# Attention and a sign-weight gate on one core: the planner of the instruction order learns when the copy of a chunk's sums is done

## The chip, the cores and the metric

One core of one Trainium2 chip runs the whole kernel in one launch. The metric is the device time of a run in microseconds (us); three runs of the kernel before are shown. A profiled execution gives the trace.

## The reference

The input x is 4 batches of 2048 tokens with 256 channels, in float32. It is normalised by token (xn). Two branches read xn: masked attention with 16 heads of 16 channels, in which query i sees keys j >= i, and a three-layer network with weights of +1 and -1, whose output passes through silu. The result is x plus the product of both branches.

```
qkv = xn @ w_qkv + b_qkv                      # 16 heads of 16
scores = q k^T / 4, and -inf where j < i
s = (softmax(scores) v, heads joined) @ w_out + b_out
h = [xn, -xn]
h = relu(s0 * h @ K0) * 2                     # K = where(k, 1, -1); to 1024
h = relu(s1 * h @ K1) * 2                     # 1024 to 1024
g = silu(s2 * h @ K2)                         # 1024 to 256
out = x + s * g
```

## The kernel before

Two phases follow each other. In the first, normalise_and_project (about the first 200 us), the tokens are normalised, q, k and v are computed chunk by chunk (a chunk is 512 tokens) and stored to scratch tensors. The second phase, attend_and_combine, holds the change.

The second phase has 16 groups (one batch, four heads), and each group goes through its four chunks of queries from the last to the first. One step is one block of 128 keys against one chunk of queries for the four heads: 4, 8, 12 and 16 steps for the four chunks, 40 a group, 640 in all. The work of TensorE (PE) has these kinds:

- **M**, the maxima: a matmul pair of queries by keys (line 1283) into two of the seven banks of ps; VectorE reads them and keeps the largest value of each row (lines 1435 and 1438). They belong to the group ahead. Once a chunk's maxima are there, they are transposed (line 1291) and written into an extra row of the queries.
- **S**, the scores: a matmul pair of keys by queries (line 1271) into two banks; ScalarE turns them into probabilities by an exponential (line 1383), kept in one of four slots of probs. Steps on the diagonal are masked on GpSimd (line 1177).
- **PV**, the products: probs times values (line 1303), accumulated over a chunk's steps in the single bank pv_ps. The fourth row group holds the sums of the softmax. After the chunk's last step, "out" on ScalarE copies pv_ps to sums_T (line 1393), from where DMAs store it ("keep"). The next chunk's first product overwrites the same bank, so it waits for that copy (semaphore out_done).
- **F**, the network: matmuls of 256 columns over 32 pieces of 256 tokens, layers L0 (line 1322), L1 (line 1325) and L2 (line 1329). Each "use" fills one bank; ScalarE reads it (relu in line 1411 for L0 and L1, an exponential and a copy in lines 1403 and 1404 for L2), and GpSimd splits a relu's output into a high and a low part (lines 1205 and 1207). After L2 come eight reciprocals on VectorE (line 1461, "recip") and one product on GpSimd (line 1215, "gate"), which makes way for the next L2's values on ScalarE.

After a batch's heads are done, its chunks are combined: loads ("fetch", "fetch_heads"), "bias" and "scale" on GpSimd, "invert" on VectorE (line 1471), "project" on PE (line 1348), then a store. For the last batch this stands in the last group.

The order of all this is one list for all engines. The class Plan makes it while the program is built: it keeps a clock for each engine and a time at which each bank is released, and at every turn it chooses among R (an S or an M pair), V (a step of PV) and F (network matmuls, two at a time, in stretches of 12 or more). The chip does not see those clocks; it sees the order, and semaphores make it safe. Each engine carries out its own part of the list in order. Three rules of the choice matter here:

```
    def products_from(self):
        t = self.products
        return self.probs_at[t] if t < self.scores // 2 else float("inf")
...
        if t == TOTAL or t >= self.products + P_SLOTS:
            return float("inf")
...
        late = behind > 0 and self.scores // 2 > TOTAL - STEPS
```

The first says from when a product may be chosen. The second is that scores run at most four steps ahead of the products. The third sets in with the last group: where the network is behind its even share of the whole, F goes on without a limit to its stretch.

Of the kernel before, what the change touches and what calls it, by code (L numbers as in the profile page):

```python
# [11 lines left out]
ACT = mybir.ActivationFunctionType  # L12
# [7 lines left out]
CHUNK = 512  # L20
# [576 lines left out]
class Plan:  # L597
# [17 lines left out]
    def __init__(self):  # L615
# [13 lines left out]
        self.probs_at, self.rows_at = {}, {}  # L629
        self.turns = []  # L630

    def emit(self, what, *args):
        self.out.append((what, *args))
        return len(self.out) - 1
# [107 lines left out]

    def products_from(self):
        t = self.products
        return self.probs_at[t] if t < self.scores // 2 else float("inf")

    def take_scores(self):
        t, pair = divmod(self.scores, 2)
# [30 lines left out]
    def take_products(self):  # L779
        g, s = divmod(self.products, STEPS)  # L780
        c, _, cols, _, stop = self.steps[s]
        self.emit("PV", g, s)
        self.clock["PE"] += 4 * cols / self.STREAM
        self.products += 1
        if stop:
            self.emit("out", g, c)
            self.clock["ACT"] = max(self.clock["ACT"], self.clock["PE"] + self.SEEN) + 0.5
            self.later(self.step() + 1, 0.0, "keep", g, c)

    def take_network(self, count):  # L790
        kind, k, q, total = self.uses[self.use]
        if self.done == 0:
            if kind == "L1" and q in (0, 2) and k + 1 < PIECES:

                self.end_span()
                self.emit("load_x" if q == 0 else "split_x", k + 1)
                self.clock["POOL"] += 0.0 if q == 0 else 1.9
            self.take(("F", self.use), "f")
        bank = self.banks["F", self.use][0]
        count = min(count, total - self.done)  # L800
        lo, self.done = self.done, self.done + count
        if self.span:
            lo = self.span[6]
        end = self.done == total
        self.span = (self.use, self.split, self.needed.get((kind, k), 0), k, kind, q, lo, self.done, end)
        self.clock["PE"] += 0.1177 * count
        self.matmuls += count
        if not end:
            return
        self.end_span()  # L810
        if kind == "L2":
            self.release[bank] = self.reads("ACT", self.clock["PE"], self.EXP, 1400)
            self.clock["POOL"] = max(self.clock["POOL"], self.release[bank]) + 1.0
            t = self.step()
            per = 2 if k + 1 < PIECES else SIG_PARTS
            for part in range(SIG_PARTS):
                self.later(t + 2 + part // per, 0.3 + 2 * (part % per) / per, "recip", k, part)
            self.later(t + 2 + SIG_PARTS // per, 0.6, "gate", k)
        else:
            if self.split >= U_SLOTS:  # L820
                self.clock["ACT"] = max(self.clock["ACT"], self.split_at[self.split - U_SLOTS])
            self.release[bank] = self.reads("ACT", self.clock["PE"], self.EXP, 640)
            self.clock["POOL"] = max(self.clock["POOL"], self.release[bank]) + 1.95
            self.split_at.append(self.clock["POOL"] + 0.1)
            self.split += 1
            self.needed["L1" if kind == "L0" else "L2", k] = self.split
        self.use += 1
        self.done = 0
# [705 lines left out]
```

## Time and profile before

| | before |
|---|---|
| median of three runs | 2479.2 us (2477.48 to 2480.41) |
| the profiled execution's own time | 2475.66 us |
| its span | 2473.9 us |
| PE busy | 2368.8 us, 96% of the span |
| VectorE busy | 1801.0 us, 73% |
| ScalarE busy | 1529.0 us, 62% |
| GpSimd busy | 910.8 us, 37% |
| mean granted clock of PE | 0.98 of full speed |

The profiled execution lies 3.5 us below the median; 1.8 us of its time lie outside the span. Busy time is the union of an engine's instructions. A matmul's end is modelled, so the start of one matmul to the start of the next says more than its duration. In the chain of work that ended last, rows of PE follow on one another, so the start of one row to the start of the next is what that stretch of matmuls took.

### The profile page before, as it was taken

The page shows a single profiled execution, that of the slowest core. Times are in us where ns is not written, and L with a number is a line of the kernel's source. Part 1 is how long each engine was busy: PE and PEld are TensorE (multiplying, and loading weights), DVE is VectorE, ACT ScalarE, POOL GpSimd, SP SyncE. Part 2 cuts the span into 40 slices and gives each one's busy share as a digit, 9 for nine tenths or more (in the row PEclk, how much of TensorE's full clock was granted, in tenths as well). Part 3 has the DMA queues.
Part 4 walks back from the last instruction along what each step waited for, and adds up shares of the span by engine and source line. Part 5 has one row for each costly group of instructions (what it writes and reads, how often), then busy time and mean ns, then how long its engine had stood idle before and what let it go on. Part 6 is the DMA issues. An engine that isn't in the chain of part 4 may idle for free.

```text
span 2473.9 us, 50994 instructions
## 1 busy us (share of the span) xinstructions
PE 2368.8 (96%) x17616; PEld 1491.4 (60%) x17616; DVE 1801.0 (73%) x4516; ACT 1529.0 (62%) x3135; POOL 910.8 (37%) x1080
## 2 busy tenths in 40 slices
PE   7999999999999999999999999999999999999885
PEld 6786655565556666656656666655666665666542
DVE  7767777777878777777777777777777777777622
ACT  5654566666666665666666665666666666666552
POOL 1004333233334344442435343442435343443432
PEclk9999999999999999999999999999999999999986
DMA  8993111110212112121312122121312121121321
GB/s 307 355 335 87 31 39 50 30 53 25 53 32 81 46 42 80 47 76 38 90 40 75 43 53 73 44 76 38 90 43 72 43 81 51 38 75 46 96 86 53
DMA packets 157805, 192.67 MB, mean 78 GB/s; under 512 B 65276, under 2 KB 102076, under 8 KB 157560
## 3 DMA queue, kind: packets, MB, share of 16 engines
q1 hardware_dynamic: 156600, 189.41, 25.1%
q8 instruction: 152, 2.49, 0.4%
q14 instruction: 93, 0.76, 0.1%
q10 hardware_dynamic: 960, 0.00, 0.0%
HBM read 112.13 MB, written 76.14 MB: 76 GB/s over the span
## 4 chain that ended last, share of the span: by engine, by line
PE 88%; DMA 4%; DVE 2%; ACT 2%; issue 2%; POOL 1%; SPq 1%; POOLq 0%; ACTq 0%; DVEq 0%
PE b_ps L1325 21%; PE b_pv_ps L1303 21%; PE b_ps L1283 15%; PE b_ps L1271 15%; PE b_ps L1329 5%; PE b_ps L1322 5%; PE b_ps L1348 3%; DMA a_xs<-L_attn_x 2%; ACT b_probs L1383 2%; PE a_qk_ps L290 1%; DVE a_stats L396 1%; DVE a_qk_parts L434 1%; PE a_v_ps L300 1%; DMA b_xs<-L_attn_x 1%; PE b_ps L1291 0%
## 5 line engine op out<-in xcount | busy, mean ns | idle before, releaser
L1383 ACT ACTIVATE b_probs<-b_ps 128x512 f32<-128x512 f32 (+3 forms) x2560 | 1187.0, 538 | 673.3 <-PE b_ps L1271 658.4
L1438 DVE TENSOR_REDUCE b_part_max<-b_ps 128x1 f32<-128x512 f32 x1536 | 964.2, 682 | 286.9 <-PE b_ps L1283 280.9
L1303 PE MATMUL b_pv_ps<-b_probs,k_vst 128*32 128x512 f32 (+3 forms) x5120 | 584.9, 542 | 48.6 <-ACT b_probs L1383 32.8
L1435 DVE CUSTOM_DVE_ANT_0 b_ps<-b_ps,k_mask 128x512 f32<-128x512 f32 (+3 forms) x1024 | 476.8, 520 | 210.2 <-PE b_ps L1283 208.0
L1325 PE MATMUL b_ps<-b_u_hi,k_w 128*128 128x256 f32 x2048 | 541.8, 300 | 0.1
L1271 PE MATMUL b_ps<-k_qst,k_kst 50*128 50x512 f32 (+3 forms) x2560 | 509.0, 413 | 3.3 <-DVE b_part_max L1435 2.5
L1325 PE MATMUL b_ps<-b_u_lo,k_w 128*128 128x256 f32 x2048 | 502.4, 281 | 0.0
L1283 PE MATMUL b_ps<-k_kst,k_qst 48*128 48x512 f32 (+3 forms) x2560 | 491.4, 409 | 3.4 <-DVE b_part_max L1438 0.9
L1325 PEld LDWEIGHTS b_ps<-b_u_hi,k_w 128*128 128x128 f32 x2048 | 390.6, 191 | 84.8 <-issue 79.7
L1205 POOL CAST b_u_hi<-b_u 128x512 fp32r<-128x512 f32 x256 | 156.8, 612 | 707.0 <-ACT b_u L1411 706.7
L1283 PEld LDWEIGHTS b_ps<-k_kst,k_qst 48*128 48x128 f32 x2560 | 235.4, 186 | 278.9 <-issue 146.1
L1325 PEld LDWEIGHTS b_ps<-b_u_lo,k_w 128*128 128x128 f32 x2048 | 389.8, 190 | 0.7
L1271 PEld LDWEIGHTS b_ps<-k_qst,k_kst 50*128 50x128 f32 x2560 | 245.3, 186 | 237.2 <-ACT b_probs L1383 73.1
L1207 POOL TENSOR_TENSOR b_u_lo<-b_u,b_u_hi 128x512 fp32r<-128x512 f32 x256 | 328.9, 1285 | 21.0
L1177 POOL TENSOR_SCALAR_AFFINE_SELECT b_probs<-b_probs 128x512 f32<-128x512 f32 x256 | 162.4, 635 | 325.6 <-ACT b_probs L1383 324.6
L1411 ACT ACTIVATE b_u<-b_ps,k_sign 128x512 f32<-128x512 f32 x256 | 176.6, 692 | 151.9 <-PE b_ps L1325 107.6
L1303 PEld LDWEIGHTS b_pv_ps<-b_probs,k_vst 128*32 128x32 f32 x5120 | 110.2, 108 | 228.1 <-issue 142.8
L1435 DVE DVE_READ_ACCUMULATOR2_ANT b_part_max<- 128x1 f32 x1024 | 144.1, 141 | 0.0
L1329 PE MATMUL b_ps<-k_w,b_u_hi 128*128 128x256 f32 x512 | 137.3, 303 | 0.0
L1322 PE MATMUL b_ps<-b_x_hi,k_w 128*128 128x256 f32 x512 | 133.7, 297 | 1.2 <-POOL b_x_lo L1195 1.1
L1329 PE MATMUL b_ps<-k_w,b_u_lo 128*128 128x256 f32 x512 | 125.9, 281 | 0.0
L1461 DVE RECIPROCAL b_sig<-b_sig 128x64 f32<-128x64 f32 x256 | 121.9, 518 | 5.2 <-POOL b_sig L1200 5.2
(101 smaller groups left out, 1852.9 us busy)
## 6 DMA issues: line engine op xcount, KB each, us to landing
qk_parts<-a_qk_parts SPq DMA_DIRECT2D x64, 512.0 KB, 4.0
k_kst<-qk_parts SPq DMA_DIRECT2D x384, 64.0 KB, 2.3
k_qst<-qk_parts SPq DMA_DIRECT2D x384, 64.0 KB, 2.3
a_xs<-L_attn_x SPq DMA_DIRECT2D x16, 512.0 KB, 5.8
xn_T<-a_xT SPq DMA_DIRECT2D x16, 512.0 KB, 5.5
v_plain<-a_v_out SPq DMA_DIRECT2D x16, 512.0 KB, 5.4
k_xf<-xn_T SPq DMA_DIRECT2D x32, 256.0 KB, 3.6
b_v_in<-v_plain SPq DMA_DIRECT2D x64, 128.0 KB, 2.6
```

The costliest lines, as they stand in the source:

```text
L1177: pool.affine_select(out=at, in_=at, pattern=[[0, GH], [-1, P]], compare_op=ALU.is_ge, fill=0.0, base=0, channel_multiplier=1).then_inc(ma ...
L1207: pool.tensor_tensor(u_lo[:, tiles], u[:, split % U_SLOTS], u_hi[:, tiles].bitcast(F32), ALU.subtract).then_inc(u_split, 1)
L1271: pe.matmul(outs[half][:, 0:cols], keys, qst[rows, c, pair, 0:cols], start=True, stop=True).then_inc(s_ready, 1)
L1283: pe.matmul(outs[j], qst[rows, c, pair, i * P:(i + 1) * P], kst[rows, k_slot(kc, g % 2), pair, k1:CHUNK], start=True, stop=True).then_inc( ...
L1303: mm = pe.matmul(pv_ps[h * VW:(h + 1) * VW, 0:cols], vst[:, kb // TT, kb % TT, h, :], probs[:, s % P_SLOTS, h, 0:cols], start=start, stop= ...
L1322: mm = pe.matmul(dst[:, tile], kept.w0[:, f, m * P:(m + 1) * P], (x_hi, x_lo)[part][:, f, :], start=first, stop=last)
L1325: mm = pe.matmul(dst[:, tile], kept.w1[:, f, m * P:(m + 1) * P], (u0_hi, u0_lo)[part][:, f, :], start=first, stop=last)
L1329: mm = pe.matmul(dst[:, tile], (u1_hi, u1_lo)[part][:, f, tile * P:(tile + 1) * P], kept.w2[:, f, :], start=first, stop=last)
L1383: act.activation(probs[:, s % P_SLOTS, h, 0:cols], ps[:, banks[place, half][0], 0:cols], ACT.Exp, scale=HD ** -0.5).then_inc(exp_done, 1)
L1411: act.activation(u[:, split % U_SLOTS], f_bank(use), ACT.Relu, scale=kept.sign[:, layer:layer + 1]).then_inc(f_read, 1)
L1435: dve.tensor_tensor_reduce(src, src, mask[:, 0:CHUNK - k0 % CHUNK], 1.0, -3.0e38, ALU.add, ALU.max, dst).then_inc(ring_read, 1)
L1438: dve.tensor_reduce(dst, src, AX_X, ALU.max).then_inc(ring_read, 1)
```

## The change

The plan gets a time `copied`, at which ScalarE's copy of a chunk's sums is done by its own clocks, and no product is chosen before it. It used to add a fixed 0.5 to ScalarE's clock and to hold no product back. A second edit stands in the network's part: at the start of every L2 use, all reciprocals and gates of the piece before that are still listed for later are put out at once. Nothing that any engine computes is different; only the order is.

```diff
@@ class Plan, __init__
+        self.copied = 0.0
@@ products_from
         t = self.products
-        return self.probs_at[t] if t < self.scores // 2 else float("inf")
+        return max(self.probs_at[t], self.copied) if t < self.scores // 2 else float("inf")
@@ take_products
         if stop:
             self.emit("out", g, c)
-            self.clock["ACT"] = max(self.clock["ACT"], self.clock["PE"] + self.SEEN) + 0.5
+            self.copied = self.reads("ACT", self.clock["PE"], self.EXP, CHUNK)
             self.later(self.step() + 1, 0.0, "keep", g, c)
@@ take_network
                 self.emit("load_x" if q == 0 else "split_x", k + 1)
                 self.clock["POOL"] += 0.0 if q == 0 else 1.9
+            if kind == "L2":
+
+                self.end_span()
+                for event in [e for e in self.side if e[2] in ("recip", "gate")]:
+                    self.side.remove(event)
+                    self.emit(*event[2:])
             self.take(("F", self.use), "f")
```

The lines of the changed kernel stand 8 lower: products are line 1311, maxima 1291, scores 1279, L1 1333, L2 1337, exponentials 1391, the copy 1401, relu 1419.

Two places show what the order becomes. The first is PE's order in the twelfth group (batch 2), where the chunk with eight steps ends and the chunk with twelve begins. Before:

```order
7295 L1271 MATMUL b_ps<-k_qst,k_kst 128x512 x2
7296 L1283 MATMUL b_ps<-k_kst,k_qst 128x512 x2
7297 L1271 MATMUL b_ps<-k_qst,k_kst 128x512 x2
7298 L1303 MATMUL b_pv_ps<-b_probs,k_vst 32x256 x4
7299 L1303 MATMUL b_pv_ps<-b_probs,k_vst 32x512 x4
7300 L1283 MATMUL b_ps<-k_kst,k_qst 128x512 x2
```

and with the change:

```order
7097 L1279 MATMUL b_ps<-k_qst,k_kst 128x512 x2
7098 L1291 MATMUL b_ps<-k_kst,k_qst 128x512 x2
7099 L1311 MATMUL b_pv_ps<-b_probs,k_vst 32x256 x4
7100 L1279 MATMUL b_ps<-k_qst,k_kst 128x512 x2
7101 L1291 MATMUL b_ps<-k_kst,k_qst 128x512 x2
7102 L1279 MATMUL b_ps<-k_qst,k_kst 128x512 x2
7103 L1311 MATMUL b_pv_ps<-b_probs,k_vst 32x512 x4
```

The first chunk's last product (256 columns) and the next chunk's first (512 columns) followed each other; now three pairs, two of scores and one of maxima, stand between them.

The second place is ScalarE's order where the last group begins, up to the copy of the group before it (the exponentials of 128 columns belong to the last group's second step). Before:

```order
883 L1411 ACTIVATE b_u<-b_ps,k_sign 128x512
884 L1383 ACTIVATE b_probs<-b_ps 128x384 x2
885 L1383 ACTIVATE b_probs<-b_ps 128x256 x4
886 L1411 ACTIVATE b_u<-b_ps,k_sign 128x512
887 L1383 ACTIVATE b_probs<-b_ps 128x512 x4
888 L1393 ACTIVATE b_sums_T<-b_pv_ps 128x512
889 L1383 ACTIVATE b_probs<-b_ps 128x128 x4
```

and with the change:

```order
863 L1391 ACTIVATE b_probs<-b_ps 128x512 x4
864 L1419 ACTIVATE b_u<-b_ps,k_sign 128x512 x8
865 L1411 ACTIVATE b_sig<-b_ps,k_gate_scale 128x512
866 L1412 ACTIVATE b_z<-b_ps,k_gate_scale 128x512
867 L1391 ACTIVATE b_probs<-b_ps 128x128 x2
868 L1401 ACTIVATE b_sums_T<-b_pv_ps 128x512
869 L1391 ACTIVATE b_probs<-b_ps 128x128 x2
```

Eight relus and one L2's two readings now stand there in one piece, without an exponential among them: on PE this is a stretch of 186 network matmuls (the rest of one L1 use, three more, four L0 uses and an L2 use), and after four pairs of maxima, two of scores and two products another of 84. The first is the only place of the program where the second edit puts anything out: eight reciprocals and a gate stand ahead of that L2.

Counted over the whole of PE's order:

| | before | with the change |
|---|---|---|
| chunk ends after which the next product follows at once (of 63) | 20 | 0 |
| stretches of scores and maxima (R) | 975 | 998 |
| stretches of products (V) | 525 | 584 |
| stretches of network matmuls (F, with transposes and projections) | 510 | 486 |
| network matmuls that stand in the last group | 288 | 538 |

## Rows read from the trace of the kernel before

**Rows 1.** The page: span and busy times of the engines.
```profile
span 2473.9 us, 50994 instructions
PE 2368.8 (96%) x17616; PEld 1491.4 (60%) x17616; DVE 1801.0 (73%) x4516; ACT 1529.0 (62%) x3135; POOL 910.8 (37%) x1080
```
**Rows 2.** Waits of PE, 230 to 2360 us: in total, times, longest.
```profile
PE b_pv_ps L1303 <- ACT b_probs L1383: 32.8, 21, 1.9
PE b_ps L1271 <- DVE b_part_max L1435: 2.5, 1, 2.5
PE b_pv_ps L1303 <- ACT b_sums_T L1393: 0.9, 1, 0.9
```
**Rows 3.** Timeline of PE around 1775 us: start us, us, instruction [idle before].
```profile
1773.66 0.64 PE L1303 MATMUL b_pv_ps<-b_probs,k_vst 128*32 128x256 f32 x8
1775.98 1.07 PE L1303 MATMUL b_pv_ps<-b_probs,k_vst 128*32 128x512 f32 x8 [1.68 <-ACT b_probs L1383]
```
**Rows 4.** Timeline of ScalarE at the same place.
```profile
1773.33 2.06 ACT L1383 ACTIVATE b_probs<-b_ps 128x512 f32<-128x512 f32 x4 [0.29 <-PE b_ps L1271]
1775.25 0.63 ACT L1393 ACTIVATE b_sums_T<-b_pv_ps 128x512 f32<-128x512 f32 x1
```
**Rows 5.** The chain of work, 1746 to 1789 us: start us, us, what.
```profile
1747.85 0.99 PE b_pv_ps L1303 x8
...
1753.59 0.43 PE b_ps L1283 x2
1754.02 0.23 PE b_ps L1271 x2
1754.25 0.23 PE b_ps L1283 x2
1754.48 1.00 PE b_pv_ps L1303 x8
...
1769.91 0.43 PE b_ps L1271 x2
1770.34 0.66 PE b_ps L1283 x4
1771.00 0.67 PE b_ps L1329 x4
...
1783.20 1.85 PE b_pv_ps L1303 x16
...
1785.73 1.61 PE b_ps L1325 x12
```
**Rows 6.** Timeline of PE: the second and the last of twelve network matmuls.
```profile
1077.05 0.28 PE L1329 MATMUL b_ps<-k_w,b_u_lo 128*128 128x256 f32 x1
...
1078.22 0.28 PE L1329 MATMUL b_ps<-k_w,b_u_lo 128*128 128x256 f32 x1
```
**Rows 7.** Busy time by stretch: stretch, length, PE, PEld, DVE, ACT, POOL busy, clock, DMA.
```profile
1500.00:2000.00 500.00, 494.89 (x3774) 304.50 (x3771) 379.28 (x948) 321.73 (x664) 196.85 (x232) 0.99 0.20 57
```
**Rows 8.** Groups of the costliest instructions: busy, mean ns, idle before.
```profile
L1207 POOL TENSOR_TENSOR b_u_lo<-b_u,b_u_hi 128x512 fp32r<-128x512 f32 x256 | 328.9, 1285 | 21.0
L1411 ACT ACTIVATE b_u<-b_ps,k_sign 128x512 f32<-128x512 f32 x256 | 176.6, 692 | 151.9 <-PE b_ps L1325 107.6 <-PE b_ps L1322 25.3 <-POOL b_u_lo L1207 17.9
L1205 POOL CAST b_u_hi<-b_u 128x512 fp32r<-128x512 f32 x256 | 156.8, 612 | 707.0 <-ACT b_u L1411 706.7
L1215 POOL TENSOR_TENSOR b_gt<-b_z,b_sig 128x512 f32<-128x512 f32 x32 | 41.1, 1285 | 6.2 <-DVE b_sig L1461 6.2
```
**Rows 9.** The chain of work where the last group begins.
```profile
2290.27 4.65 DMA b_sums<-sums
...
2294.94 0.55 DVE b_sums L1471
```
**Rows 10.** Waits of PE, 2360 us to the end.
```profile
PE b_ps L1348 <- POOL b_heads_T L1237: 19.3, 3, 8.0
PE b_pv_ps L1303 <- POOL b_probs L1177: 14.3, 3, 7.6
```

## The prediction

> **What bounds the kernel now.** I read the page first, for who is busy: PE for 2368.8 of 2473.9 us, VectorE for 73% and ScalarE for 62% of it [rows 1]. PE is the bound, and the other two have slack on the average. Then PE's waits, for what PE could win: between 230 and 2360 us it waits for 36.2 us altogether in the three largest rows, and 33.7 of them, in 22 waits, stand before a product (line 1303) [rows 2]. The row names ScalarE's exponentials (line 1383), and that name has to be looked at closely. The timeline at one such place shows it: PE ends the eight matmuls of a chunk's last product at 1774.30, then sits idle for 1.68 us until the next chunk's first product at 1775.98 [rows 3]. ScalarE has four exponentials in its queue until 1775.39, and behind them the copy of pv_ps from 1775.25 to 1775.88; the product starts 0.10 after the copy's end [rows 4]. So it is the copy (line 1393) that PE waits for, and the exponentials are what the copy waits behind. The 22 waits fit the 20 chunk ends at which the order has nothing between the two products, with two or three where it has too little. Last I read the chain of work, from start to start, for what the stretches of matmuls cost.
>
> **Term 1, the waits removed.** All 20 places get other work: in the first place shown, three pairs, 0.9 us. The 33.7 us go, as far as the filler is long enough: −33.7.
>
> Some fillers are short. After the change seven chunk ends have only two to four pairs in between (0.7 to 1.1 us by the pairs of [rows 5]), where the wait from the last product's end was 1.7. That leaves 0 to 1.0 us at each of seven, 0 to 7; since the plan holds the product back by a clock that counts ScalarE's queue, I take +2.
>
> **Term 2, more and shorter stretches.** Work that is taken in between cuts other stretches. PE's order has 59 more stretches of products, 23 more of scores and maxima, and 24 fewer of the network. What each costs is read from the chain. One step of products takes 0.99, two in a row 1.85, not 1.98 [rows 5]: a stretch more costs 0.13. Three pairs take 0.43, 0.23 and 0.23 [rows 5]: the first pays 0.20. Twelve network matmuls take 1.61 [rows 5], and from the second to the last start of twelve it is 1.17 for ten intervals [rows 6], 0.117 each, so 1.40 without the change of kind: 0.21. The sum is 59 × 0.13 + 23 × 0.20 − 24 × 0.21 = 7.7 + 4.6 − 5.0 = +7.3. On each of these edges the trace shows the lost time beside the row, whatever its reason. The Trainium skill (TensorEngine Tiling (Array Packing), Key Properties) has a rule that speaks against this change: changing the tiling mode drains TensorE. Its page on TensorE (TensorE: Matmul & The Clock Gate, Single matmul latency) gives a fixed part of a warm matmul's latency of 398 cycles at 2.4 GHz, 166 ns; with a full drain at each of the 58 more changes of kind, an estimate by these two pages is 9.6 us, and the sum would be 2.3 us less of a gain. The rows give 7.3, and the trace agrees that each change is paid for.
>
> **Term 3, thinner groups.** The network falls behind: 538 instead of 288 of its matmuls stand in the last group, so the 15 groups before it have 250 fewer, 250 × 0.117 = 29.3 us of PE work moved later. That is neutral as long as PE stays the bound in those groups. But the same maxima and scores then have less filler between them, and seven banks to go round. VectorE is busy for 379 of 500 us there and ScalarE for 322 [rows 7], so with 2 us less of filler a group (137 us) neither is near its limit on the average; what can come is the short wait for a bank. One is in the rows: three pairs took 1.09 (1769.91 to 1771.00) where three others took 0.89 [rows 5], 0.20 more. Below, the cost is 0, or a gain: three-pair stretches fall from 600 to 550, and at 0.20 each that would be −10. Above, it is all 29.3, when the thinned groups take as long as before. The nearest rows (0.20 per stretch, at some thirty of the 82 stretches that are new) give +6, which I take.
>
> **Term 4, the last group.** At its start 186 network matmuls run in one piece, and ScalarE's second order shows what is behind it. From the end of the last L1 use: its relu takes 0.69 and its split on GpSimd 0.61 + 1.29 = 1.90 [rows 8], so 2.8 with the hand-over. Then come four L0 uses, 0.94 of PE each but 1.90 of GpSimd: 2.8 + 7.6 = 10.4. The gate of the piece before, put out there by the second edit, is behind them: +1.29 [rows 8] = 11.7. Only then may ScalarE read the L2 result (twice 0.69, a price as of line 1411 [rows 8]), and behind that stand two exponentials and the copy, 0.5 + 0.63 [rows 4] = 14.2. PE needs 3.8 + 3.8 for L0 and L2 and some 2.3 for the pairs and the product in between, and stands before the next chunk's first product at 9.9. That is a new wait of +4.3, once. Without the flush ScalarE would wait for a gate that is listed behind it. In exchange the fetch of the first chunk to be combined is issued ahead of that stretch, and its invert behind: before, the DMA of the sums landed at 2294.92 with VectorE's invert waiting for it, the pairs of maxima behind the invert [rows 9], and PE idle for 2.5 [rows 2]. Behind 22 us of network it has long landed: −2.5. The end of the group (33.6 us of waits for the last combines and masks [rows 10]) has the same order in both but for a few rows, and stays.
>
> **The sum.** −33.7 + 2 + 7.3 + 6 + 4.3 − 2.5 = −16.6. Against the profiled execution's 2475.7 that is 2459.1. It lies 3.5 below the median of the runs, so the median should come to 2479.2 − 16.6 = **2462.6**. Everything else (first phase, the engines' instructions and their number, the DMAs) is the same and costs nothing.
>
> **Rivals.** (a) *The network's debt is not neutral: slower.* If the thinned groups become bound by the hand-over of banks to VectorE and ScalarE, Term 3 is 29.3 instead of 6: −16.6 + 23.3 = +6.7, 2486. It decides against the change from 22.6 on, that is when over three quarters of the moved work are not won back. For it: each place between two products now takes pairs ahead of time, and scores can be no more than four steps ahead of the held-back product. Against it: VectorE's 76% and ScalarE's 64% [rows 7]. The last group's slice of the profile would then show the whole 29 us on top of a main stretch of unchanged length. (b) *It does not do what it says.* The plan's clocks are not the chip's; where ScalarE runs later than planned, PE still arrives too early. If half the waits stay, −16.6 + 17 = 0, 2479. Against it: the fillers are mostly 2.5 us (twelve network matmuls and three pairs), more than the 1.7 of the wait. (c) *A larger gain.* With Term 3 at 0 and no rest at the short places: −24.6, 2455; with three-pair stretches fewer as well down to 2445.
>
> **How the numbers follow.** The forecast with (c), a gain of 5 to 34 us, gets 0.75; (b) and other ways to about no change 0.12; (a) 0.13. Within 0.2% (5 us) is about what a measurement of this kernel can tell from no change. The range goes from 2446, the gain of (c) with all of its parts, to 2484, between (b) and (a), which leaves out the worst of (a).
>
> **What would show it.** In the changed profile: PE's waits before products between 230 and 2360 us under 8 us instead of 33.7; the span from 230 us to the last group's start shorter by some 45 (29 of moved work and the gain); a single wait of 3 to 5 us before a product some 25 us into the last group; no wait of 2.5 for the maxima there; the same 34 us at the end. I would be wrong if waits of PE's weight loads for exponentials and maxima grew by 20 us and more, or if that first stretch were shorter by 20 us or less.

## The result, and the profile after

| | before | with the change |
|---|---|---|
| median of the runs | 2478.34 us (2473.18 to 2480.41, 4 runs) | 2451.16 us (2444.74 to 2456.07, 4 runs) |
| profiled execution | 2475.66 us, span 2473.9 | 2456.07 us, span 2454.3 |

The ratio is 0.9892, with a 95% interval from 0.9860 to 0.9924: 27 us faster. The forecast was 16.6 us faster, on the right side and within its range, but short of the measured gain. The two profiled executions differ by 19.6 us, and a further execution of the changed kernel (below) lies 25.1 us under the first profile of before: the same program varies by more than I had thought, and that turned out to be the missing part.

The page of the changed kernel, its span and busy times, answers [rows 1]:

```profile
span 2454.3 us, 50994 instructions
PE 2378.8 (97%) x17616; PEld 1487.3 (61%) x17616; DVE 1795.6 (73%) x4516; ACT 1525.9 (62%) x3135; POOL 912.7 (37%) x1080
...
L1311 PE MATMUL b_pv_ps<-b_probs,k_vst 128*32 128x512 f32 (+3 forms) x5120 | 593.9, 544 | 10.4 <-POOL b_probs L1185 10.1
```

PE sat idle for 48.6 us before its products, and now for 10.4, nearly all of it at the very end. PE's waits between 230 and 2312 us, where the last group's first third ends, answer [rows 2]:

```profile
PE b_ps L1279 <- ACT b_z L1412: 4.4, 1, 4.4
PE b_ps L1299 <- DVE b_part_max L1446: 1.5, 5, 0.3
PE b_ps L1291 <- ACT b_probs L1391: 1.0, 4, 0.4
```

No row of products is among the first ones: the 33.7 us are gone. In their place stands the single wait of the last group that the prediction had worked out, 4.4 us. From 2312 us to the end, the waits answer [rows 10]:

```profile
PE b_ps L1356 <- POOL b_heads_T L1245: 15.6, 3, 7.2
PE b_pv_ps L1311 <- POOL b_probs L1185: 10.1, 2, 7.5
PE b_ps L1279 <- DMA k_qst<-b_max_parts: 3.8, 1, 3.8
```

Those came to 33.6 and come to 29.5. The wait of 3.8 for a load of queries is new.

The matmuls of the trace can be laid on the order one by one. By that, from the second phase's first matmul to the last group's first scores, before took 2102.3 us and the change 2054.6: 47.7 less, of which 29.3 are the 250 network matmuls that were moved, and 18.4 a gain. The last group up to the last projection took 179.1 and takes 207.9: 28.8 more for 29.3 of moved work. That these two agree within 1 us is luck of this pair of profiles. The 28.8 is a net of the moved work, a new wait, a wait that is gone and a shorter end. Between the second profiles of both kernels (experiments 1 and 5), the first part is 49.5 us shorter and the last group only 22.1 longer. What the two pairs show is that the moved work costs no more in the last group than it took before.

The place of [rows 3, 4] with the change, from a second profile of the changed kernel (r_after), in the chain of work:

```profile
1727.09 0.57 PE b_pv_ps L1311 x8
1727.66 0.42 PE b_ps L1279 x2
1728.08 0.03 issue
1728.11 0.49 PE b_ps L1291 x2
1728.60 0.40 PE b_ps L1279 x2
1729.01 0.99 PE b_pv_ps L1311 x8
```

and in ScalarE's timeline:

```profile
1727.26 1.09 ACT L1391 ACTIVATE b_probs<-b_ps 128x512 f32<-128x512 f32 x2
1728.21 0.62 ACT L1401 ACTIVATE b_sums_T<-b_pv_ps 128x512 f32<-128x512 f32 x1
```

From one product to the next it is 1.92 us instead of 2.32 (1775.98 − 1773.66 in [rows 3]), and three pairs are done in between. Note that these three pairs take 0.45, 0.49 and 0.41 from start to start, where three pairs took 0.43, 0.23 and 0.23 in [rows 5]. PE isn't idle in the profile there, but it is not at its rate either: part of the wait has moved into the pairs, which wait for their banks.

### The profile page after: what moved, and what is told of

It is laid out like the page before. It is cut to its first block, busy times and chain, and to the rows that moved or that the text cites. A ratio compares the mean times of both kernels' runs of the same rounds, so it can differ in the third digit from the quotient of the medians.

```text
span 2454.3 us, 50994 instructions
## 1 busy us (share of the span) xinstructions
PE 2378.8 (97%) x17616; PEld 1487.3 (61%) x17616; DVE 1795.6 (73%) x4516; ACT 1525.9 (62%) x3135; POOL 912.7 (37%) x1080
## 4 chain that ended last, share of the span: by engine, by line
PE 88%; DMA 4%; DVE 3%; POOL 2%; issue 1%; ACT 1%; SPq 1%; POOLq 0%; ACTq 0%; DVEq 0%
PE b_pv_ps L1311 21%; PE b_ps L1333 21%; PE b_ps L1291 15%; PE b_ps L1279 14%; PE b_ps L1330 5%; PE b_ps L1337 5%; DMA a_xs<-L_attn_x 3%; PE b_ps L1356 3%; PE a_qk_ps L290 1%; DVE a_stats L396 1%; DVE a_qk_parts L434 1%; ACT b_probs L1391 1%; DMA b_xs<-L_attn_x 1%; PE b_ps L1299 1%; DMA out<-b_xs 0%
## 5 line engine op out<-in xcount | busy, mean ns | idle before, releaser
L1311 PE MATMUL b_pv_ps<-b_probs,k_vst 128*32 128x512 f32 (+3 forms) x5120 | 593.9, 544 | 10.4 <-POOL b_probs L1185 10.1
L1291 PE MATMUL b_ps<-k_kst,k_qst 48*128 48x512 f32 (+3 forms) x2560 | 505.2, 416 | 5.7 <-ACT b_probs L1391 1.0
L1279 PE MATMUL b_ps<-k_qst,k_kst 50*128 50x512 f32 (+3 forms) x2560 | 499.2, 408 | 10.0 <-ACT b_z L1412 4.4
L1330 PE MATMUL b_ps<-b_x_lo,k_w 128*128 128x256 f32 x512 | 125.9, 280 | 0.0
```

Source lines behind the costliest of these rows:

```text
L1279: pe.matmul(outs[half][:, 0:cols], keys, qst[rows, c, pair, 0:cols], start=True, stop=True).then_inc(s_ready, 1)
L1291: pe.matmul(outs[j], qst[rows, c, pair, i * P:(i + 1) * P], kst[rows, k_slot(kc, g % 2), pair, k1:CHUNK], start=True, stop=True).then_inc( ...
L1311: mm = pe.matmul(pv_ps[h * VW:(h + 1) * VW, 0:cols], vst[:, kb // TT, kb % TT, h, :], probs[:, s % P_SLOTS, h, 0:cols], start=start, stop= ...
L1330: mm = pe.matmul(dst[:, tile], kept.w0[:, f, m * P:(m + 1) * P], (x_hi, x_lo)[part][:, f, :], start=first, stop=last)
```

## The experiments

Theory A was that of the prediction: the waits go, and the added stretches are paid for. Its rival B was that the gain comes from the new interleaving or from the chip. Times of kernels stand against runs of the kernel before on the same chip.

### 1. The change again: r_after

No edit.

> The changed kernel again, on the chip of the three runs beside it. Theory A (the gain is the waits of PE for the copy that go, less what the shorter stretches cost): 17 to 27 us faster than before, as in the runs so far. Theory B (much of the gain is luck of the new interleaving or of the chip): anywhere from 5 to 30, and not in step with the run below that only moves the products.

2449.29 us (5 runs) against 2480.58 (9 runs), ratio 0.9878 (0.9854 to 0.9903). The two profiles of the same program differ by 5.5 us of span (2448.8 against 2454.3). They run in step, within 0.4 us, up to 1028 us into the program; by 1289 the second is 5.5 ahead, and from there they are in step again. The stretches of 10 us of the first profile (stretch, length, busy of PE, PEld, DVE, ACT, POOL, then the granted clock, DMA share, GB/s) show where:

```profile
1030.00:1040.00 10.00, 9.71 (x82) 5.57 (x80) 8.43 (x36) 7.63 (x19) 8.35 (x12) 1.00 0.28 75
1040.00:1050.00 10.00, 10.00 (x45) 3.06 (x45) 6.15 (x12) 5.71 (x11) 0.00 (x0) 0.50 0.05 12
1050.00:1060.00 10.00, 10.00 (x74) 7.01 (x78) 6.79 (x11) 5.59 (x13) 2.82 (x4) 0.98 0.52 155
```

For 10 us PE was granted half its clock, the lower of its two levels, and began 45 matmuls instead of some 80, while the page calls it wholly busy. The second profile has the full clock at the same place. This gave theory C: part of a kernel's time, and of its spread, is PE's granted clock.

### 2. Only the products moved: e1_moved

The plan of before, then a function over its list. Nothing but the 20 products moves (banks are renamed to the new places of the list).

```diff
-    order, banks = Plan().made()
+    order, banks = moved(*Plan().made(), False)
+def moved(order, banks, back):
+    ...
+            # a product that follows the copy at once
+            if n < len(items) and not back and not any(kinds.get(i[1][0]) for i in items[at + 1:n]):
+    ...             # goes behind the next two stretches of other kinds
+                items.insert(m - 1, items.pop(n))
```

> The order of before, in which only the 20 first products that followed the copy at once are put behind the next two stretches of other work (about 2.3 us each); nothing else moves, and the last group has no long piece of network. Theory A: the 33.7 us of waits go, 19 more stretches of products cost 2.5, a rest of 2 stays: 28 to 31 us faster than before, thus more than the change itself. Theory B: under 10 us faster, since ScalarE's exponentials wait in the moved product's place.

2446.58 us (4 runs), ratio 0.9867 (0.9843 to 0.9892): 34 us faster, no less than the change. So the gain is the 20 moved products; the other thousands of places that the plan rearranged, the thinner groups and the fuller last group add nothing to it that these runs can tell. B falls. Its profile shows PE's waits between 230 and 2240 us:

```profile
PE b_pv_ps L1336 <- ACT b_probs L1416: 1.9, 2, 1.0
PE b_ps L1316 <- ACT b_probs L1416: 1.1, 3, 0.5
PE b_ps L1304 <- ACT b_probs L1416: 0.6, 1, 0.6
```

But a sum of waits removed (30.6 of the 33.7 lie before 2240 us) less 2.5 should not give 34. Something else was won, and something lost: laid on the order, waits for banks ahead of a pair of scores or maxima grew from 26 to 36 us, although this order has as much network in each group as before. (The level depends on what one takes as the time of a pair that does not wait. The growth of 10 hardly does.)

### 3. The products put back into the changed order: e2_back

```diff
-    order, banks = Plan().made()
+    order, banks = moved(*Plan().made(), True)     # each first product right behind the copy
```

> The changed order, with every chunk's first product put back right behind the copy (62 places with nothing in between). Theory A: about 60 waits of 1.0 to 1.9 us, 60 to 110 us in all, less 57 stretches of pairs and 60 of products that merge again (19 us): 40 to 90 us slower than the change, 20 to 70 slower than before. Theory B: within 15 us of the change.

2622.3 us (4 runs), ratio 1.0576 (1.0550 to 1.0602): 142 us slower than before and 173 slower than the change, about twice the 90 that I expected at most. The waits between 230 and 2240 us:

```profile
PE b_pv_ps L1344 <- ACT b_probs L1424: 58.4, 40, 2.2
PE b_pv_ps L1344 <- POOL b_probs L1218: 9.8, 5, 2.7
PE b_ps L1324 <- ACT b_probs L1424: 9.3, 20, 0.7
PE b_pv_ps L1344 <- ACT b_sums_T L1434: 8.9, 8, 2.0
```

The direction is A's: with 62 places instead of 20 the waits before products come to 77 us. Yet 173 is more than waits. In this profile PE's clock record holds 16 stretches at the lower level between 230 and 2240 us, 85 us in all. Compared start to start with the same transitions elsewhere, the matmuls in them cost 39 us extra. A further 50 are waits ahead of pairs of scores and maxima. Half of them are idle time (the third line above is one such row), the other half the page counts as busy. So A had left out two things, the lower clock (theory C) and the waits of the pairs.

### 4. The copy planned still later: e5_more

```diff
-            self.copied = self.reads("ACT", self.clock["PE"], self.EXP, CHUNK)
+            self.copied = self.reads("ACT", self.clock["PE"], self.EXP, CHUNK) + 0.6
```

> The change with the copy's end planned 0.6 us later (fillers of 3.8 us on the mean, 2 short ones, 588 network matmuls in the last group). Theory A: no wait is left to be won, so the same as the change within 5 us, or a little slower for the 50 matmuls more that are moved to the last group. Theory B: the order is another throw of the dice, 10 us or more from the change to either side.

2452.37 us (4 runs), ratio 0.9890 (0.9866 to 0.9914), 3 us above the change on the same chip: the same. Holding the product longer wins nothing more, and an order that differs almost everywhere costs nothing either.

### 5. The kernel before again: r_before

No edit.

> The kernel before, run and profiled once more, to see what varies from run to run. Theory C (each wait of PE for the copy can be followed by a stretch in which PE is granted half its clock; the first profile had six such stretches between 230 and 2240 us, each right behind such a wait): again 22 waits of 33 to 34 us, some 3 to 10 stretches at the lower clock, every one behind one of those waits, and the times spread by 10 us with them. Rival: the lower clock comes at places without a wait as well.

2478.81 us (10 runs, 2471.81 to 2498.56), ratio 0.9987 (0.9961 to 1.0014). The waits repeat to a tenth: 33.0 in 21 and 0.9, 0.5. The lower clock does not. The first profile has six such stretches between 230 and 2240 us (from 417, 588, 1359, 1499, 1639 and 2052 us, 27 us in all), the second has four (416, 1221, 2044, 2184; 17 us). All ten stand behind one of the waits for the copy, and each time behind one of over 1.6 us, of which a profile has 13 up to there. In e2_back there are 27 such waits before the last group, and a stretch at the lower clock follows 13 of them. The place at 1359 us, in the first profile:

```profile
1349.00:1359.00 10.00, 8.30 (x74) 5.34 (x76) 7.03 (x12) 7.10 (x15) 3.73 (x5) 1.00 0.17 50
1359.00:1366.00 7.00, 7.00 (x32) 4.29 (x24) 2.30 (x4) 2.06 (x4) 2.51 (x3) 0.51 0.12 26
```

and in the second:

```profile
1349.00:1359.00 10.00, 8.30 (x68) 5.05 (x60) 6.45 (x11) 6.51 (x13) 4.32 (x5) 1.00 0.22 65
1359.00:1366.00 7.00, 7.00 (x56) 4.97 (x56) 5.56 (x10) 4.85 (x9) 2.98 (x4) 1.00 0.16 38
```

Both have PE idle for 1.7 us of the first 10. In the one, PE then runs at half its clock and begins 32 matmuls in 7 us, in the other 56. Start to start, the lower clock costs 11.5 us of the first profile and 7.7 of the second. The expected rival, a lower clock without a wait, does not occur in this kernel between 230 and 2240 us, but it does in the changed one (experiment 1, and 3.4 us at 1166 us in the same profile): at the first place PE ran products and pairs alone, without network matmuls, from 1034.7 to the fall at 1040.1. The Trainium skill (TensorE: Matmul & The Clock Gate, HAM oscillation — how this bites in real kernels) says that idle gaps between bursts of matmuls bring the clock down, and names gaps longer than any of these waits. The ten places agree in kind, with gaps of 1.7 to 1.9 us. The Trainium skill (TensorE: Matmul & The Clock Gate, What's actually happening) also makes the level of the clock a matter of how busy PE has been. By the profile PE was busy for 9.71 of the 10 us up to 1040 us, and the second profile passes the same place at the full clock. What brought the clock down there was not tried.

The times of single runs show the price of the clock as well. Each run has its mean granted clock on record, and for 47 runs of the kernel before (all those beside the experiments) it goes from 0.970 to 0.982. The seven runs at 0.981 took 2475.0 us on the mean, the seven at 0.975 took 2487.6: 12.6 us more for 30 us more at the lower level (0.006 × 2 × 2480), or 0.4 us for each. All runs with the products moved have 0.982 to 0.989. An estimate from this: against the trend of the 47 runs, the nine runs of the change lie 13 to 16 us below what the kernel before would take at the same clock, so about half of the gain of 27 to 31 us is the clock. The first profile of before, at 0.980, is one of the faster runs, and shows less of it.

The 17 further runs of this same kernel beside these ten have a median of 2484.68 us, 6 us higher. So a difference of that size between two kernels shows nothing by itself.

### 6. A shorter filler: e11_short

As e1_moved, the products put behind one stretch instead of two.

```diff
-                        if len(stretches) == 2:
+                        if len(stretches) == 1:
```

> The order of before, the 20 first products put behind only the next one stretch of other work, the three (or two) pairs of 0.9 us. About half of each wait stays: 20 waits of some 0.8 us, 16 in all. If a wait costs its own length and nothing more, 17 less 2.6 for 20 stretches more = 14 us faster than before. Theory C (a long wait also brings stretches at half the clock, 8 to 12 us of the kernel before): the lower clock is gone with waits that short, and it is 22 to 26 us faster, three quarters of what moving them behind two stretches gives.

2449.38 us (6 runs), ratio 0.9881 (0.9861 to 0.9902): 29 us faster. I expected 16 us of waits to be left; in its profile 2.1 us stand before products up to 2240 us (0.9, 0.8 and 0.4), because the rest of the wait now lies in the pairs. Its chain of work at the place of [rows 3]:

```profile
1751.15 0.47 PE b_ps L1304 x2
1751.62 0.00 ACTq L1415
1751.62 0.04 issue
1751.67 0.46 ACT b_probs L1416
1752.13 0.04 issue
1752.17 1.08 ACT b_probs L1416 x2
1753.25 0.02 issue
1753.28 0.49 PE b_ps L1304 x2
1753.77 0.11 issue
1753.88 0.50 PE b_ps L1304 x2
1754.38 1.01 PE b_pv_ps L1336 x8
```

PE goes at the pace of ScalarE's exponentials here, which free the banks. A group of the steady part with a single wait of 1.7 us and no lower clock took 137.1 us in the kernel before, and takes 136.1 here and 136.0 with the product behind two stretches: 1.0 to 1.1 of 1.7 is won, whichever filler. The lower clock is nearly gone before the last group (one stretch of 3.4 us).

The measured 29 does not decide between A and C by itself. The 14 of A and the 22 to 26 of C both rested on 16 us of waits being left. With 2.1 left, A would have given some 26 (30.6 − 2.1 − 2.6). The trace decides: from 230 us to the last group's first scores this profile is 27.3 us shorter than the first of before. Of that, some 9 us are the lower clock, and the 28.5 us of waits that went gave the other 18, some 0.6 of their length, as in the single group.

### 7. The gate put out earlier: e7_gate

```diff
-            if kind == "L2":
+            if kind == "L2" or kind == "L1" and q == 2 and self.scores // 2 >= TOTAL - STEPS:
```

> The change, with the reciprocals and the gate of the piece before put out two uses earlier in the last group, ahead of GpSimd's splits of the first layer. If ScalarE's wait for that gate is what PE's wait of 4.4 us at 2260 us comes from, that wait goes and the kernel is 3 to 4 us faster than the change; if it is the network's length in one piece, the wait stays.

2441.93 us (6 runs), ratio 0.9836 (0.9811 to 0.9862), by the medians 7 us below the change, where 3 to 4 was expected. What the wait of 4.4 us came from is seen in the changed kernel's own timeline, first GpSimd:

```profile
2257.29 1.27 POOL L1215 TENSOR_TENSOR b_u_lo<-b_u,b_u_hi 128x512 fp32r<-128x512 f32 x1
2258.51 1.26 POOL L1223 TENSOR_TENSOR b_gt<-b_z,b_sig 128x512 f32<-128x512 f32 x1
```

then ScalarE:

```profile
2259.81 0.69 ACT L1411 ACTIVATE b_sig<-b_ps,k_gate_scale 128x512 f32<-128x512 f32 x1 [4.36 <-POOL b_gt L1223]
2260.40 0.68 ACT L1412 ACTIVATE b_z<-b_ps,k_gate_scale 128x512 f32<-128x512 f32 x1
```

then PE:

```profile
2256.10 0.64 PE L1311 MATMUL b_pv_ps<-b_probs,k_vst 128*32 128x256 f32 x8
2261.13 0.48 PE L1279 MATMUL b_ps<-k_qst,k_kst 50*128 50x128 f32 x2 [4.39 <-ACT b_z L1412]
```

This is the chain of Term 4, link by link. From the relu of the last L1 use (2248.15 us) to the end of the gate it took 11.6 us, where the prediction had 11.7. That the wait came out right as well is partly luck: PE stood still after 8.6 us instead of 9.9, and was released by the L2 reading at 12.9, ahead of the copy, instead of at 14.2. With the gate earlier the wait is gone, and the busy time of PE and its clock from 2240 to 2300 us go from (r_after)

```profile
2240.00:2300.00 60.00, 55.09 (x414) 41.93 (x413) 27.80 (x69) 26.96 (x57) 40.63 (x44) 0.91 0.13 35
```

to (e7_gate)

```profile
2240.00:2300.00 60.00, 59.47 (x474) 44.47 (x474) 34.33 (x80) 28.79 (x61) 41.05 (x46) 1.00 0.14 44
```

So the wait of 4.4 us brought a stretch of 10.2 us at the lower clock with it, from 2253.2 us on in r_after. The spans differ by 8.5 us (2448.8 and 2440.3): the wait, and about as much again for the clock.

### 8. The network kept up: e6_even

```diff
-            if network and (self.matmuls - self.begun < self.STRETCH or late):
+            if network and (self.matmuls - self.begun < (self.STRETCH if behind < 60 else 24) or late):
```

> The change, with the network's stretches doubled wherever it is over 60 matmuls behind, so that 344 instead of 538 of its matmuls stand in the last group. If moved network work costs (the term for thinner groups, 6 us in the prediction), 3 to 8 us faster than the change. If it is neutral, the same within 3.

2447.46 us (6 runs), ratio 0.9846 (0.9821 to 0.9870). Against the change's 0.9878 the intervals overlap, so a gain isn't shown. Its profile tells more. The 194 matmuls are 22.7 us of work (0.117 each). The last group became 7.6 us shorter than their leaving accounts for (no long piece, hence no wait for the gate), and the part ahead of it took 4.0 longer than they account for, instead of less. About 3 of these 4.0 are idle time and the lower clock, above all two new waits of 2.0 and 1.3 us and 3.4 us at the lower level behind the first. Waits for banks are 36 us against 33 in r_after. Fuller groups thus did not lower the waits of the pairs.

### 9. The last group's loads earlier: e8_early, e9_both, e10_all

e8_early is e1_moved with this edit; e9_both is the change with this edit and that of e7_gate; e10_all is e9_both with that of e6_even.

```diff
-    chunks += [(base, NCHUNK - CPB - 1, COMBINE),
+    chunks += [(base - 8, NCHUNK - CPB - 1, COMBINE),
```

> The order of before with the 20 products moved, and the loads and the combine of the last batch but one's last chunk eight steps earlier. The run with the products moved had a wait of 4.2 us of PE for VectorE at the start of the last group, and one of 3.9 before a product: with the loads landed in time both go, 4 to 8 us faster than that run (2446.6), thus 38 to 42 us faster than before. If the waits only move, the same within 2.

> The change with the gate put out earlier and the combine of the last batch but one's last chunk eight steps earlier. With the change the loads land behind the long piece of network anyway, so only the gate counts: the same as the run with the gate alone (2441.9) within 3 us. If the loads matter here too, up to 5 faster.

> The same with the network's stretches doubled wherever it is over 60 matmuls behind. The run with those alone had no long piece of network, no wait of 4.4 and no low clock at the start of the last group, and stood within 2 us of the change; its waits that are left there (2.0 and 1.3 us) are of other kinds. If the three edits add up: 2438 to 2442. If thinner groups are neutral, it is the same as the run with two of them.

e8_early: 2442.75 us (5 runs), ratio 0.9831 (0.9805 to 0.9856); the wait of 4.2 for VectorE is gone, that before a product went from 3.9 to 5.9, and its span is 4.5 below e1_moved's (2441.5 and 2446.0). e9_both: 2443.12 (4 runs), 0.9853 (0.9829 to 0.9877); its profile again has 10.2 us of lower clock from 1038 us on, the place of experiment 1. e10_all: 2441.78 (4 runs), 0.9849 (0.9826 to 0.9872), with the shortest span of all profiles, 2438.7. All three came out within what was expected, or within 1 us of it, except that the wait before a product did not go. The three and e7_gate can't be told apart. All four beat the kernel before by about 35 to 43 us, and by their medians the change by 6 to 8, which lies at the edge of what these runs resolve.

## Why the prediction was right, and where it was off

- **What PE waited for.** Right: the copy behind the exponentials. e1_moved shows that the 20 products alone carry the gain, and the second edit plus the new clock formula without the hold leave the order word for word as it was, which the built order shows. The hold without the second edit was not run.
- **Term 1, waits of 33.7.** As a wait it went altogether (0.3 is left in the changed profile up to the last group), but as a price it was mis-sized, and this is the step that failed. A wait of 1.7 us was counted at its length. It costs less and more. It costs less, because 1.0 to 1.1 of 1.7 is won in a group without a lower clock; the rest comes back where pairs wait for their banks (10 us in e1_moved), probably because VectorE and ScalarE no longer have the pause to catch up in. It costs more, because behind such a wait PE is sometimes granted half its clock for 3.4 or 6.8 us. That cost 11.5 us of the profile of before, and none was in the sum; I had the granted clock of 0.98 in the table and did not ask where the missing part lay. The second profile of the change has no such stretch before the last group, the first has two (6 us).
- **Term 1, the rest of 2.** Too high; hardly any wait is left at the short places, as e11_short explains: the pairs in the filler take up the wait.
- **Terms 2 and 3.** The sum was fitting, one reason was not. Laid on the order, waits for banks grew by 6.7 us in r_after (6.3 in the first profile), as the 6 that I took; but in e1_moved, with no group thinner, they grew by 10, and e6_even did not lower them. They came with the waits' end, not with thin groups. What is left for the stretches and all else is 10 us (25.4 gained from 30.6 of waits and 11.5 of clock, less 6.7), where 7.3 and 2 stood. Laid on the order by kind of transition, about 5 of the 10 are the added stretches, and about 3 are short waits before pairs and transposes that the page shows. So the 7.3 was somewhat high.
- **Term 4.** The chain was right. That its sum came within a tenth (4.3 and 4.4) is partly luck: PE stood before a pair of scores for want of a bank, not before a product, and both its arrival and its release came 1.3 us earlier than worked out. Its price was 8.5 with the lower clock. The wait of 2.5 went as forecast. The waits of the group's end, which I had left unchanged, came to 33.6 and 36.2 us in the two profiles of before and to 29.5 and 28.9 with the change.
- **Rivals.** (a) fell: the 29.3 us were saved where they came from, and made the last group 22 to 29 us longer, the new wait included. (b) fell: the plan's clock was good enough; 0.6 us more changed nothing (e5_more). (c) had the size but not the reason, so its hit is luck.

All in all: −16.6 forecast; the profiles give −19.6 and −25.1, and the medians −27 and −31. At an equal clock the runs give an estimated 13 to 16 (experiment 5), near the 16.6. What the sum lacked was the clock.

## What to carry to other kernels

Where PE is the bound and waits for another engine at a place that is known, put other work of PE there by moving the waiting instruction. Two or three pairs were enough here (e11_short), and the rest of the plan did not have to change (e1_moved). Count a wait of PE at more than its length if the granted clock falls behind it, and look for the clock's low stretches before summing: they also tell what part of the spread between runs can be removed. When work is postponed, look at what stands ahead of it in the slower engine's queue at the place where it piles up: the one wait that the change brought cost 8.5 us with its clock, the length of five of those that it removed.

## What was not expected of the hardware

- Behind a wait of PE of 1.7 to 1.9 us the granted clock fell to half for 3.4 or 6.8 us in 10 of 26 cases (two profiles with 13 waits of over 1.6 us each up to 2240 us), mostly at different ones in each execution, and in these two profiles behind none of the shorter waits. In e2_back it followed 13 of 27 such waits and also one of 1.1 and one of 1.5 us. Behind the wait of 4.4 us it was 10.2 us in both profiles, behind one of 4.2 in e1_moved 3.4 us, behind one of 4.0 in e5_more 6.8 us.
- It also fell for 10.2 us (at 1040 us in one profile of the change and at 1038 in e9_both), and for 3.4 or 6.8 us at three more (at 1166 us in the same profile of the change, at 908 in e5_more, at 638 in e11_short), where PE had no idle time above 0.31 us just before; why is open. Ahead of each of these five PE had run products and pairs without a network matmul for 3 to 6 us. That isn't enough by itself: r_after has the same stretch at 1035 us, for 12 us, at the full clock. The one such stretch of e6_even, at 2005 us, stands behind a wait of 2.0 us.
- A matmul that waits for its bank counts as busy in the page. Three pairs that take 1.65 us instead of 0.9 in e11_short (1752.68 to 1754.33 us) show no idle time of PE above 0.1 us.
